# Local attention in a decoder kernel: half-token transposes of the softmax weights, maxima as steps of their own, and a new order of steps

## The reference, cut to what matters

```python
x = x + _L0_attn_ref(_layernorm(x), ...)   # A, gated linear attention
x = x + _L0_xattn_ref(_layernorm(x), ...)  # B, cross attention
x = x + _L0_ffn_ref(_layernorm(x), ...)    # C, mixture of experts
x = x + _L1_attn_ref(_layernorm(x), ...)   # D, local attention: the stage of this change
x = x + _L1_xattn_ref(_layernorm(x), ...)  # E
x = x + _L1_ffn_ref(_layernorm(x), ...)    # F
```

```python
qkv = (x @ Wqkv.T).reshape(B, T, 3, H, hd).transpose(2, 0, 3, 1, 4)
q = q * cos + _rotate_half(q) * sin
k = k * cos + _rotate_half(k) * sin
scores = jnp.einsum('bhqd,bhkd->bhqk', q, k) / jnp.sqrt(hd)
allow = (j <= i) & (jnp.abs(i - j) <= 128)
scores = jnp.where(allow, scores, -jnp.inf)
y = jnp.einsum('bhqk,bhkd->bhqd', jax.nn.softmax(scores, axis=-1), v)
return y.transpose(0, 2, 1, 3).reshape(B, T, C) @ Wproj.T + bproj
```

## Time and profile before

| | |
|---|---|
| runs, median (lowest to highest) | 2528.76 us (2523.03 to 2533.08) |
| profiled execution, own time | 2528.92 us |
| its span | 2527.1 us |
| PE, PEld busy | 2246.4 us (89%), 1868.0 us (74%) |
| DVE, ACT, POOL busy | 1596.7, 1165.5, 737.1 us |
| stage D, from its first instruction to its last matmul | about 1388 to 1695 us |

### The profile page before, as it was taken

The page is one execution under the profiler, slowest core; times in us unless marked ns, Lnnn a source line. Parts: engine busy times, 40 slices in busy tenths (PEclk is TensorE's granted clock), DMA queues, the critical chain, the costliest instruction groups (busy, mean ns, idle before and its releaser), DMA issues. The chain is left out here.

```text
span 2527.1 us, 63640 instructions
## 1 busy us (share of the span) xinstructions
PE 2246.4 (89%) x26627; PEld 1868.0 (74%) x26627; DVE 1596.7 (63%) x3513; ACT 1165.5 (46%) x3240; POOL 737.1 (29%) x866
## 2 busy tenths in 40 slices
PE   5798989999898999946997689989997899999998
PEld 4677877777785888835886466667776788888887
DVE  6666676667653566546773455655666777777776
ACT  4435444443423777612553366656664233333332
POOL 2334243333423444331664523420101001110110
PEclk9799999999999999967999799999998899999999
DMA  5001010100101100021442300000000000000001
GB/s 162 1 11 36 27 36 11 36 27 11 66 3 60 62 19 19 19 76 39 123 108 47 88 2 2 2 2 2 2 2 20 13 26 26 26 21 24 26 7 34
DMA packets 87966, 83.44 MB, mean 33 GB/s; under 512 B 27264, under 2 KB 83456, under 8 KB 86272
## 3 DMA queue, kind: packets, MB, share of 16 engines
q1 hardware_dynamic: 81536, 70.98, 8.9%
q0 software_dynamic: 6144, 8.39, 2.0%
HBM read 68.71 MB, written 10.65 MB: 31 GB/s over the span
## 5 line engine op out<-in xcount | busy, mean ns | idle before, releaser
L2676 PE MATMUL bank<-f_XH,f_wp 128*128 128x512 f32 x1088 | 364.6, 396 | 5.9 <-DVE f_XL L2786 5.9
L797 DVE SCALAR_TENSOR_TENSOR a_acc<-a_praw,a_convw,a_acc 128x256 f32<-128x256 f32 x345 | 206.2, 599 | 99.2 <-ACT a_acc L957 91.0
L2676 PEld LDWEIGHTS bank<-f_XH,f_wp 128*128 128x128 f32 x1088 | 208.4, 192 | 48.5 <-issue 5.0
L2676 PEld LDWEIGHTS bank<-f_wp,f_Hp 128*128 128x128 f32 x1632 | 214.3, 191 | 27.5 <-DVE X L2813 16.0
L2676 PE MATMUL bank<-f_wp,f_Hp 128*128 128x256 f32 x1632 | 218.5, 283 | 16.2 <-DVE X L2813 15.4
L2676 PE MATMUL bank<-f_XL,f_wp 128*128 128x512 f32 x544 | 215.9, 397 | 0.0
L2860 POOL TENSOR_TENSOR f_wp<-wa,f_wp 128x768 fp32r<-128x768 f32 x34 | 62.9, 1850 | 521.5 <-ACT f_wp L2826 521.5
L2811 DVE SCALAR_TENSOR_TENSOR X<-bank,f_w,X 128x256 f32<-128x256 f32 x512 | 211.4, 476 | 0.0
L2849 ACT ACTIVATE f_Hp<-f_H 128x512 fp32r<-128x512 f32 x136 | 85.9, 632 | 223.8 <-DVE f_H L2798 223.8
L2847 ACT ACTIVATE f_G<-bank 128x512 f32<-128x512 f32 x136 | 81.3, 598 | 165.4 <-PE bank L2676 165.4
L594 PE MATMUL bank<-XT,wa 128*128 128x256 f32 x512 | 155.2, 434 | 0.3 <-ACT a_acc L957 0.3
(11 more groups left out here) (390 smaller groups left out, 5520.2 us busy)
## 6 DMA issues: line engine op xcount, KB each, us to landing
wa<-in_c_w SPq DMA_DIRECT2D x64, 256.0 KB, 3.4
wa<-in_f_gu SPq DMA_DIRECT2D x34, 256.0 KB, 2.7
wb<-grown SPq DMA_DIRECT2D x4, 1536.0 KB, 7.0
a_KQg<-grown SPq DMA_DIRECT2D x4, 1536.0 KB, 6.5
wa<-in_f_d SPq DMA_DIRECT2D x34, 128.0 KB, 2.8
a_E<-decays SPq DMA_DIRECT2D x16, 256.0 KB, 4.0
X<-in_x SPq DMA_DIRECT2D x4, 512.0 KB, 5.2
wa<-in_a_wqkv SPq DMA_DIRECT2D x1, 2048.0 KB, 8.8
```

The costliest lines, as they stand in the source:

```text
L797: i = v.e.scalar_tensor_tensor(A_, praw[:, c, :, j:j + BT_], convw[:, c, j:j + 1], A_, ALU.mult, ALU.add)
L2676: i = t.e.matmul(out_, lhsT[x], rhs[y], start=n == 0 and k == 0, stop=n == 2 and k == nk - 1, skip_group_check=True)
```

## The change: what it does

1. **Turns in halves.** `turn` g, h (h = 0, 1) now covers four heads. Each 128x128 transpose becomes two transposes of 64 tokens each. One is on rows 0 to 63 and the other on rows 64 to 127 of the array, and they write two different banks. ACT copies the bank of the first halves and DVE that of the second, for every turn.
2. **Maxima apart.** The maxima become steps `max`. Two stand before the second turn. The third and fourth stand later, each directly ahead of its exponentials.
3. **Second turn ahead of the first exponentials.** On ACT the copies of `flip` and of the second turn now come before the group's first exponentials.
4. **Odd steps.** `values` comes first, then `project`, then `across` (before: `project`, `across`, `values`).
5. **Start of the stage.** Only two layer norms stand before the loop. The others are spread: `norm` at the start and `ln` at the end of steps 2 to 7. `project` 1 comes behind the first keys. The rotation of tile 0 is done by DVE. POOL's clearing memsets come first of all its work. The load of the bias `d_bo` has a semaphore of its own, so that TensorE does not wait for it.

The new order and the new turn on TensorE:

```diff
-            lns = [[("stat", "D", i)] * (i < 4) + [("norm", "D", i - 1), ("ln", "D", i - 1)] * (i > 0) for i in range(5)]
-            order = lns[0] + lns[1] + [("project", 0), ("project", 1)] + lns[2] + [("keys", 0, 0), ("keys", 0, 1)] + lns[3] + lns[4]
+            order = [("stat", "D", 0), ("stat", "D", 1), ("norm", "D", 0), ("ln", "D", 0), ("norm", "D", 1), ("project", 0)]
+            order += [("ln", "D", 1), ("keys", 0, 0), ("keys", 0, 1), ("project", 1)]
...
-                order += turn[0:2] + [("mix", g - 2)] * (0 <= g - 2 < G)
-                order += scores + exps[0:1]
+                order += [("stat", "D", g + 1)] * (1 <= g < 7) + [("norm", "D", g)] * (2 <= g < 8)
+                order += turn[0:1] + [("mix", g - 2)] * (0 <= g - 2 < G) + scores
+                order += [("flip", n)] * (g % 2 == 0 and 0 <= n < NT) + maxima[0:2] + turn[1:2] + exps[0:2]
                 if g % 2 == 0:
...
+                    order += across + [("keys", m + 1, 0), ("keys", m + 1, 1)] * (m + 1 < NT) + maxima[2:3] + exps[2:3]
+                    order += [("out", n)] * (0 <= n < NT) + maxima[3:4] + exps[3:4]
...
+                    order += [("values", m)] * (m < NT) + [("project", m + 2)] * (m + 2 < NT) + across + maxima[2:3] + exps[2:3]
+                    order += maxima[3:4] + exps[3:4]
...
-                                i = t.e.transpose(pair(b.ap)[:, j, kt * P:(kt + 1) * P],
-                                                  Pm[of(g, r)][:, j, kt * P:(kt + 1) * P], ident)
...
+                                    for half, rows_ in enumerate(halves):
+                                        b = at[s + (half,)]
+                                        i = t.e.transpose(by_group(b.ap)[:, r, j, kt, :],
+                                                          Pm[of(g, 2 * h + r)][rows_, j, kt * P:(kt + 1) * P],
+                                                          ident[rows_, rows_], tile_position=(rows_.start, 0))
```

How the copies are divided, and the start:

```diff
-                    elif what == "turn" and s[2] < 2:
+                    elif what == "turn":      # ACT; DVE has the same with half 1
...
+                        c.e.activation(PT[of(g, 2 * h) // 2][:, :, :, kts, halves[0]], by_group(b.ap)[:, :, :, kts, :],
+                                       ACT.Copy).then_inc(b.emptied, 1)
...
-                y.e.dma_start(bo[:, :], on_all("d_bo")).then_inc(w_in, 16)
+                y.e.dma_start(bo[:, :], on_all("d_bo")).then_inc(bo_in, 16)
...
-                        t.wait_ge(w_in, 48)
+                        t.wait_ge(w_in, 32)
...
+                    elif s == ("project", 0):
+                        rotate(v, 0)
```

More of the change, by code:

```diff
@@ L1990, in stage_d @@
+            order += [("ln", "D", 1), ("keys", 0, 0), ("keys", 0, 1), ("project", 1)]
             for g in range(G + 3):
                 m, n = g // 2, g // 2 - 2
-                turn = [("turn", g - 1, r) for r in range(4)] if 0 <= g - 1 < G else []
-                scores, exps = ([(what, g, r) for r in range(4)] if g < G else [] for what in ("score", "exp"))
+                turn = [("turn", g - 1, h) for h in range(2)] if 0 <= g - 1 < G else []
+                scores, maxima, exps = ([(what, g, r) for r in range(4)] if g < G else [] for what in ("score", "max", "exp"))
@@ L2002, in stage_d @@
                 else:
[L2003 to L2006, removed]
+                    order += [("values", m)] * (m < NT) + [("project", m + 2)] * (m + 2 < NT) + across + maxima[2:3] + exps[2:3]
+                    order += maxima[3:4] + exps[3:4]
+                order += [("ln", "D", g)] * (2 <= g < 8)
@@ L2028, in stage_d @@
                     i = s[-1]
-                    max_ready.mark(*s[1:])
+                elif what == "turn":
+                    for half in range(2):
+                        at[s + (half,)] = banks[4 + turns % 4]
+                        at[s + (half,)].turn(*k, half)
+                        turns += 1
+                    continue
                 else:
@@ L2054, in tensor @@
                     what, b = s[0], at.get(s)
-                    if what in ("exp", "bias", "shut", "stat", "norm"):
+                    if what in ("max", "exp", "bias", "shut", "stat", "norm"):
                         continue
@@ L2107, in tensor @@
                         emptied(t, "values", n)
-                        for r in range(4):
-                            emptied(t, "turn", g, r)
+                        for h in range(2):
+                            for half in range(2):
+                                emptied(t, "turn", g, h, half)
                         for j in range(2):
@@ L2222, in scalar @@
                         if g > 1:
-                            filled(c, "turn", g - 2, r)
+                            for half in range(2):
+                                filled(c, "turn", g - 2, r // 2, half)
                         c.wait_ge(max_ready.sem, max_ready.at[g, r])
```

102 lines of the change are left out of this document (56 added, 46 removed).

## The result

The changed kernel takes 2485.49 us, the median of four runs (2483.76 to 2488.95). The kernel before took 2527.95 beside it (2523.03 to 2533.08). The ratio is 0.9834, with an interval of 0.9811 to 0.9856. The forecast was 2508, with a range that ended at 2490. So the gain is 42 us where 21 were forecast.

The account below looks back on a forecast made before the run. PE was taken to bound stage D's loop, with small waits, after a start that waits. Start 11.6 plus loop 9.7 gave 21 us off 2528.9, so 2508 us; range 2490 to 2528, the forecast's own 2499 to 2516.

Parts of the forecast that it names:

- the price of the half turns: Stage D turns: sixteen half transposes cost 0.87 us, like eight full ones, priced from L739; range 0.64 to 1.74.
- the forecast's 9.7: Loop gain over steps 8 to 27: ten pairs at 0.75 us plus five times 0.44 for layer norms.
- The changes of shape: Around half turns on PE: five new tile-shape changes a pair at 0.10 us each, adding 0.5 us.
- The waits: Loop: first keys' wait goes, PE waits 0.6 us for QT before the odd step's first turn.
- This just fits. I add 0.1: Fourth score bank's mask: due at 10.8 us, last exponentials done at 10.7, so 0.1 us added.
- With `values` first ... nothing waits: Odd step: the projection's 1.72 us cover the copies, so the step takes 8.1 us against 8.31.
- The pair: Loop: an even and an odd step together take 16.5 us, 0.75 less than before.
- The start: Stage D up to step 8: begins at 1472.5 against 1484.1, a gain of 11.6 us.
- The turns get cheaper: Rival on stage D turns: a block costs 0.64 us, 14 to 18 us more gain, about 2492; chance 0.12.
- The halves do not overlap: Rival on stage D turns: a block costs 1.74 us, adding 52 us, about 2560; chance 0.09.

Follow-up runs that it names:

- full_turns: Changed kernel with full 128x128 turns instead of half turns, new order kept: 2494.22 us, 0.9898 of the kernel before.
- matmul_turns: Changed kernel with its half turns made by an ordinary float32 matmul against the identity instead of a transpose: 2555.90 us, 1.0121 of before.
- old_odd_full: Changed kernel with the odd steps' old order (project, across, values) and full 128x128 turns: 2487.30 us, 0.9859 of before.
- old_odd: Changed kernel with the odd steps' old order (project, across, values): 2480.07 us, 0.9841 of before; again 2471.13 us, 0.9806.
- the third profile: Third profiled run of the changed kernel, no edit: median 2489.68 us, 0.9858 of before.
- halves_alone: Kernel before with only the half turns and their divided copies, old start and old loop order: 2522.44 us, 1.0006 of before.
- exps_first: Changed kernel with the first two exponentials ahead of flip and the second turn: 2508.44 us, 0.9944 of before.
- maxima_together: Changed kernel with all four maxima ahead of the second turn: 2491.73 us, 0.9885 of before.
- maxima_before_across: Changed kernel with the odd step's last two maxima and exponentials ahead of project and across: 2493.49 us, 0.9892 of before.

## Why the prediction was wrong

The step that failed is the price of the half turns. The forecast let them cost what full turns cost, and 5 x 0.10 = 0.5 us a pair on top. full_turns shows where that leads. Without the 0.5 the forecast's pair would be 16.0 us or a little more, and full_turns measured 15.9. Its ten pairs of steps 8 to 27 took 155.6 us, 13.9 less than the 169.6 of before, where the forecast's 9.7 and ten times 0.5 make 14.7. So the new order was judged about right in sum, though its waits fell elsewhere (below). The halves then took another 3.4 us off these pairs (152.3), where the forecast had them add up to 5. The steps behind them gained 4.0 us, and the forecast had nothing there. Piece by piece:

- **The price of a block failed.** The step was "In the first the weight load has the new width, and I take its price", with 0.87 from L739. It took 0.64, the price of L1348, the other row. I had matched the width of the weights, and should have matched the kind of instruction: both are sixteen rows in the trace, but L739's are eight matmuls of two instructions each. matmul_turns shows it. Here are the groups of weight loads, each shape apart, three of the changed kernel and the last of matmul_turns; behind the count stand busy us and the mean ns of one:

```profile
L1348 PEld LDWEIGHTS bank<-wide,b_P 64*77 64x77 f32 x1024 | 44.6, 151 | 14.1 <-POOL b_P L1509 13.5
L2081 PEld LDWEIGHTS bank<-wide,d_P 64*128 64x128 f32 x960 | 36.1, 141 | 19.7 <-issue 14.2 <-ACT d_QT L2258 1.6 <-ACT d_PT L2278 1.1
L739 PEld LDWEIGHTS bank<-a_ud,a_kn 64*128 64x128 f32 x512 | 32.4, 194 | 2.8 <-DVE a_ud L908 0.7
...
L2081 PEld LDWEIGHTS bank<-wide,d_P 64*128 64x128 f32 x1920 | 114.1, 190 | 16.6 <-issue 12.9 <-ACT d_QT L2259 1.5 <-ACT d_PT L2279 0.2
```

  77 and 128 weights of a transpose load alike (151 and 141 ns). The ordinary one of the same 64 by 128 takes 194, and 190 in the very place of the half turns. The Trainium skill says that the load lasts by its columns (TensorE: Matmul & The Clock Gate, LDWEIGHTS). By that rule 77 columns would be faster than 128, and these rows don't show it. The same page of the Trainium skill, in its Terms, names a transpose mode of the weight load and the matmul on trn2 as four times faster for FP32. The measured block differs by 1.93 / 0.64 = 3.0.
- **The changes of shape** were forecast at 0.5 us a pair, and the halves do cost about that at the groups around them (old_odd_full). But before's own cost on the way out of a turn, which I had carried along (0.97 and 0.93 beside 0.87), is gone. PE's need in a pair came to 14.3 us (15.57 less the waits 0.72 and 0.54), against 15.66. Of the 1.35 difference, 4 x 0.23 = 0.92 is the block, 0.26 that way out, and 0.17 is left over. The waits give 0.4 of it back, so the pair is 0.9 us shorter than forecast.
- **The waits.** The first `keys` wait for nothing, and the first turn of the odd step waits some 0.54 us for `QT` (forecast 0.6). Both are right. "This just fits. I add 0.1" for the fourth mask was wrong: 0.72. DVE divides ahead of the last maxima, as the step says, but `across` comes late because `values` stands first:

```profile
1509.75 0.38 PE L2142 MATMUL bank<-wide,d_OT 128*128 128x128 f32 x2
1510.17 0.21 DVE L2220 RECIPROCAL d_rec<-bank 128x8 f32<-128x8 f32 x1 [1.70 <-PE bank L2142]
1510.41 0.29 DVE L2221 TENSOR_TENSOR d_AO<-bank,d_rec 128x128 f32<-128x128 f32 x1
```

  From the start of `across` to the mask that waits it takes 3.34 us (1509.75 to 1513.09). The forecast's own figures give 2.9 (from 8.1 less 0.32 to 10.7). DVE is done with the division only 0.95 us after `across` has started. With full turns the wait is 0.49 already, so the layout was tight by more than I gave it, and cheaper turns brought the mask forward into more of it.
- **"With `values` first ... nothing waits"** was counted as part of the gain. It is a loss, as old_odd shows, of 7.4 us from step 8 on (189.8 to 182.4), and of more at the start.
- **The pair** came to 15.5 to 15.6 us, not 16.5. The loop's 9.7 became 21.3 in two parts. The ten pairs gained 17.3 (169.6 to 152.3). Two of them, around the first tile of the second batch row, were shorter before (14.30 and 15.66) and gained only 0.2 and 1.3. The last steps, where I counted nothing, gave the other 4.0.
- **The start** was right: 11.0 against 11.6 (8.8 in the third profile), with its landmarks within 1 to 2 us, and POOL's rotation as the wait ahead of the second keys.
- **The rivals.** "The turns get cheaper" had the block right (0.64), and I gave it 0.12 because of the 77 columns. Its 2492 is nearer than my 2508, but partly by luck: it took the cheap block to be worth 14 to 18 us over full price, and full_turns gives 3.4 to 4.3. Stage D's gain of 32.3 would make 2496.6 from before's profile. The rest down to 2485 is variation outside the stage, mostly ahead of it, and not explained by the change: the three measurements of it give 42, 35 and 34 us below their own kernel before. "The halves do not overlap" fell: a block would have taken 1.74.
- **Where the gain is.** Start 8 to 11 us. Order of the loop with the new division of the copies, at full turns, 17 (full_turns). Halves 4 on top of it, and nothing without it (halves_alone). The values in front take 7 away, and more at the start.

## What to carry to other kernels

Take the price of an instruction from a row of the same kind of operation first, and of the same shape second: for float32, count how many instructions the trace shows for one of the program's. In this loop a cheaper operation on the engine that bounds it was worth nothing while that engine waited for copies: the copies had to go ahead of the long work on their engine first, and only then did the saving count. When several orders are changed at once, undo each alone, since one of them can be eating what the others bring.

## What was not expected of the hardware

The granted clock at the start of the stage differs between programs that do the same work up to there. The stretch from 10 to 20 us behind the last sum, first of the changed kernel, then of old_odd (columns as above):

```profile
1389.47:1399.47 10.00, 7.78 (x19) 4.02 (x19) 2.89 (x5) 1.79 (x3) 0.00 (x0) 0.50 1.06 308
```

```profile
1391.09:1401.09 10.00, 7.35 (x34) 4.13 (x37) 2.90 (x5) 2.76 (x5) 0.42 (x1) 0.79 0.99 290
```

The order of instructions is the same until step 1, yet in old_odd the clock left the 1.2 GHz level earlier, and the projection that takes 3.62 us after takes 2.64 there. In these 10 us the clock was 0.50 in all three profiles of the changed kernel and in exps_first, maxima_together, old_odd_full and matmul_turns. It was 0.62 in full_turns, 0.79 in maxima_before_across, and 0.77 and 0.79 in the two profiles of old_odd.

The clock seems to be worth 3 to 4 us of a start. maxima_before_across has a start 4.2 us shorter than the changed kernel's (80.4 against 84.6), with no gain from step 8 on. full_turns, whose blocks are dearer, has one 3.2 us shorter. old_odd_full's start is 3.2 us longer than old_odd's (80.5 against 77.3), but the price of its turns is in that too. So some 3 to 4 of the 7.3 us by which old_odd's start is shorter than the changed kernel's may come from the clock, and no run separates them. What decides it stays open.
